# Attention kernel: who adds the causal mask to the diagonal maxima, VectorE or TensorE

## The chip, the cores and the metric

The kernel runs on one core of a Trainium2 chip. The metric is the device time of one execution in microseconds. TensorE (PE in the rows; PEld are its weight loads), VectorE (DVE), ScalarE (ACT), GpSimd (POOL) and the DMA queue of SyncE (SP) run side by side and wait for one another on semaphores.

## What is computed

One transformer layer on x of shape 4 x 2048 x 256, in float32: layer norm, causal attention with 16 heads of 16 dimensions, a residual, layer norm, a two-layer network with ternary weights and a squared ReLU, a residual. The part that matters here:

```python
qkv = x @ W_attn + b_attn
q, k, v = jnp.split(qkv, 3, axis=2)
...
scores = jnp.einsum('bhqd,bhkd->bhqk', qh, kh) * scale
causal = jnp.tril(jnp.ones((S, S), dtype=bool))
scores = jnp.where(causal, scores, -jnp.inf)
probs = jax.nn.softmax(scores, axis=-1)
out = jnp.einsum('bhqk,bhkd->bhqd', probs, vh)
```

## The kernel before

The program has four stages in a row: the preparation of the weights, the projection to q, k and v (`build_qkv`), attention (`build_attention`) and the network (`build_mlp`). Attention handles 16 units, each one batch entry and a group of `GH` = 4 heads. In a unit the queries come in `NCH` = 4 chunks of `CH` = 512.

The softmax needs the maximum of each query's row before the exponentials. So the scores are formed twice. Once they are formed with the queries across the partitions, into `ps_m`, only to find the maxima. Later they are formed with the keys across the partitions, into `ps_s`, with the negated maxima as two further rows of the product; ScalarE takes the exponential of each bank of 512 columns into the ring `probs`, and TensorE multiplies `probs` by v into `ps_acc`. A float32 product with v is two instructions, so eight weight loads stand in the trace for four heads.

The maxima are found in items, listed in `MAXES` (line 88), 68 to a unit. An item fills two banks of `ps_m`, one for each head r of a pair, at partitions 0 to 47 and 64 to 111 of the array, so that the two products run at once. There are two slots of two banks (`SLOTS`), so TensorE forms item k only after VectorE is done with item k-2 (`slot_freed`). In chunk c there are 8c full items of one piece of 512 columns, and then five items on the diagonal: two for query tile 3 (one piece of 512 columns), two for query tile 2 with tile 0 (pieces of 384 and 128), and one for query tile 1 (two pieces of 256, one for each pair of heads). Below they are called D3, D2 and D1.

`reduce_max` (line 970) is VectorE's part. A full item is one `tensor_reduce` over 1024 elements. For an item on the diagonal each piece of each head takes one custom instruction that adds `mask` and takes the maximum (line 983), followed by a read of the accumulator. Before the first of them VectorE waits on `slot_freed` for its own last item, since `sums_masked` is written again.

`order` (line 117) fixes the sequence on all engines. Between two pairs of score banks stands one item, and behind it half of the product with v for the step three earlier. So TensorE's rhythm is scores, item, values. The items run `LEAD` = 40 ahead of the scores: while the scores of a unit are formed, the items are those of its last chunk and then those of the next unit. The first 40 items of the first unit run ahead of all scores (`OPENING`); here TensorE has nothing but items to form. For the last unit no items are left after its own.

The mask is made by GpSimd in the preparation (line 244). In `build_qkv` ScalarE issues `load_ones` (line 544), four DMAs, between the copies of the first transposed chunk and the root of the second chunk's layer norm (`take_root(act, 1)`).

Of the kernel before, what the change touches and what calls it, by code (L numbers as in the profile page):

```python
# [26 lines left out]
ALU = mybir.AluOpType  # L27
# [70 lines left out]
ROWS_BEHIND = 6  # L98

# [91 lines left out]
def build_prep(nc, io, keep):  # L191

    with ExitStack() as ctx:
# [42 lines left out]
        def _(pool):  # L236
# [7 lines left out]
            pool.affine_select(out=keep["mask"][:, CH - P:], in_=keep["mask"][:, CH - P:], compare_op=ALU.is_ge, fill=NEG,  # L244
                               base=0, pattern=[[-1, P]], channel_multiplier=1).then_inc(masked, 1)

# [83 lines left out]
        def _(pe):  # L330
            pe.wait_ge(loaded, 16 * 9)
            pe.wait_ge(masked, 2)
# [168 lines left out]
class Shared:  # L501
# [3 lines left out]
    def __init__(self, nc, ctx):  # L505
# [6 lines left out]
        self.ones = t.sb("ones", [ROW, ROW])  # L512
        self.ones_set, self.fixed_in = t.sem("ones_set"), t.sem("fixed_in")
# [38 lines left out]
FIXED = 2 * MROWS  # L552
# [4 lines left out]
def build_qkv(nc, io, keep, scr, sh):  # L557

    with ExitStack() as ctx:
# [96 lines left out]
        def _(act):  # L656
            norm.take_root(act, 0)
            copy_high(act, xn_t[0], ps_t, xt_ready, xt_copied, 0)
            act.wait_ge(sh.ones_set, 1)
# [67 lines left out]
def build_attention(nc, io, keep, scr, sh):  # L727

    with ExitStack() as ctx:
# [4 lines left out]
        probs, stack_in = sh.probs, sh.stack_in  # L734

        sums_masked = t.sb("sums_masked", [P, 4, CH])
        maxes = [t.sb(f"maxes{i}", [P, 2, PAIRS, TT, NCH]) for i in range(2)]
        neg_max = [t.sb(f"neg_max{i}", [P, 2, PAIRS * TT]) for i in range(2)]
        max_parts = [t.sb(f"max_parts{i}", [P, 2, MROWS, PAIRS * TT], F32R) for i in range(2)]
        max_rows = [t.sb(f"max_rows{i}", [MROWS * GH * TT, P], F32R) for i in range(2)]  # L740
# [228 lines left out]
        def _(dve):  # L969
            def reduce_max(n, k):  # L970
# [3 lines left out]
                if pieces[0][2] < c:  # L974
                    (p, tt, i, _, _), = pieces
                    last = dve.tensor_reduce(maxes[c % 2][:, :, p, tt, i], ps_m[:, 2 * slot:2 * slot + 2], AX.X, ALU.max)  # L976
                else:

                    if NM * n + k > 0:
                        dve.wait_ge(slot_freed, NM * n + k)  # L980
                    for p, tt, i, col, width in pieces:
                        for r in range(2):
                            last = dve.tensor_tensor_reduce(sums_masked[:, 2 * pieces.index((p, tt, i, col, width)) + r, 0:width], ps_m[:, 2 * slot + r, col:col + width],  # L983
                                                            keep["mask"][:, CH - width:], 1.0, NEG, ALU.add, ALU.max,
                                                            maxes[c % 2][:, r, p, tt, i:i + 1])
# [37 lines left out]
        def _(pe):  # L1023
            def form_max(n, par, k):
# [364 lines left out]
def build_layer(nc, io):  # L1389
    with ExitStack() as ctx:  # L1390
# [11 lines left out]
            "mask": t.sb("mask", [P, CH]),  # L1402
# [41 lines left out]
```

## Time and profile before

| what | us |
|---|---|
| time, median of 3 runs | 2164.73 |
| lowest, highest | 2157.74, 2168.49 |
| the profiled execution, its own time | 2183.39 |
| its span from first to last instruction | 2181.5 |
| attention with scores, one unit of sixteen | 92.1 |

The profiled execution is 0.9% longer than the median. Durations of the rows are read against its own time. In a row of the timeline stand the start, the time to the end of the last of the merged instructions, the engine, the line, the operation, the output and inputs, partitions and elements, the count and, in brackets, how long the engine had been idle and what released it. In rows of PE and PEld the shape is partitions and rows of the product, then the elements.

### The profile page before, as it was taken

The page shows a single profiled execution, that of the slowest core. Times are in us where ns is not written, and L with a number is a line of the kernel's source. Part 1 is how long each engine was busy: PE and PEld are TensorE (multiplying, and loading weights), DVE is VectorE, ACT ScalarE, POOL GpSimd, SP SyncE. Part 2 cuts the span into 40 slices and gives each one's busy share as a digit, 9 for nine tenths or more (in the row PEclk, how much of TensorE's full clock was granted, in tenths as well). Part 3 has the DMA queues.
Part 4 walks back from the last instruction along what each step waited for, and adds up shares of the span by engine and source line. Part 5 has one row for each costly group of instructions (what it writes and reads, how often), then busy time and mean ns, then how long its engine had stood idle before and what let it go on. Part 6 is the DMA issues. An engine that isn't in the chain of part 4 may idle for free. (4 is left out here: it accounts for less than half of the span.)

```text
span 2181.5 us, 45406 instructions
## 1 busy us (share of the span) xinstructions
PE 2043.4 (94%) x17133; PEld 1099.8 (50%) x17133; DVE 1878.0 (86%) x3965; ACT 1497.3 (69%) x2800; POOL 475.9 (22%) x635
## 2 busy tenths in 40 slices
PE   3999599999999999999999999999999949999998
PEld 2877244444444344444444444444444328888887
DVE  7987889999999899999999999999999218988886
ACT  1333078888888788888888888888888725555554
POOL 0000011110111111111110111101111026776674
PEclk8999579999999999999999999999999759999999
DMA  3799121211212121121311212212120022232320
GB/s 94 281 314 321 50 50 37 73 55 54 55 37 67 48 63 49 48 63 37 78 46 51 56 37 77 53 52 56 37 73 29 12 82 81 85 102 83 88 78 30
DMA packets 162363, 168.10 MB, mean 77 GB/s; under 512 B 74064, under 2 KB 102240, under 8 KB 162144
## 3 DMA queue, kind: packets, MB, share of 16 engines
q1 hardware_dynamic: 154112, 157.72, 24.6%
q10 hardware_dynamic: 8032, 7.47, 1.2%
q8 instruction: 135, 2.21, 0.4%
q14 instruction: 84, 0.69, 0.1%
HBM read 95.77 MB, written 67.63 MB: 75 GB/s over the span
## 5 line engine op out<-in xcount | busy, mean ns | idle before, releaser
L955 ACT ACTIVATE probs<-ps_s 128x512 f32<-128x512 f32 x2176 | 1181.6, 596 | 261.1 <-PE ps_s L1067 237.3
L976 DVE TENSOR_REDUCE maxes<-ps_m 128x2 f32<-128x1024 f32 x768 | 910.6, 1218 | 71.3 <-PE ps_m L1036 65.7
L1088 PE MATMUL ps_acc<-probs,vs 128*32 128x256 f32 (+1 forms) x8696 | 709.9, 399 | 14.2 <-ACT acc_sb L933 14.2
L1067 PE MATMUL ps_s<-qs,ks 50*128 50x512 f32 (+3 forms) x2560 | 579.4, 453 | 0.4 <-ACT probs L955 0.4
L1036 PE MATMUL ps_m<-ks,qs 48*128 48x512 f32 (+3 forms) x2560 | 505.9, 401 | 36.7 <-DVE maxes L983 12.9
L983 DVE CUSTOM_DVE_ANT_0 sums_masked<-ps_m,mask 128x512 f32<-128x512 f32 (+3 forms) x1024 | 446.9, 488 | 49.9 <-PE ps_m L1036 4.6
L1067 PEld LDWEIGHTS ps_s<-qs,ks 50*128 50x128 f32 x2560 | 255.5, 187 | 420.4 <-ACT probs L955 375.1
L1088 PEld LDWEIGHTS ps_acc<-probs,vs 128*32 128x32 f32 x8696 | 174.3, 109 | 329.2 <-issue 222.9
L1036 PEld LDWEIGHTS ps_m<-ks,qs 48*128 48x128 f32 x2560 | 253.1, 191 | 156.5 <-DVE maxes L983 92.5
L893 POOL TENSOR_SCALAR_AFFINE_SELECT probs<-probs 128x512 f32<-128x512 f32 x256 | 159.3, 637 | 729.2 <-ACT probs L955 725.4
L1242 POOL TENSOR_TENSOR hid<-square,hid 128x512 fp32r<-128x512 f32 x128 | 175.9, 1383 | 105.7 <-DVE square L1253 92.8
L881 POOL CAST max_parts<-neg_max 128x16 fp32r<-128x16 f32 x64 | 12.7, 198 | 604.2 <-DVE neg_max L990 604.2
L1315 ACT ACTIVATE relu<-ps_h 128x512 f32<-128x512 f32 x128 | 76.4, 597 | 90.0 <-PE ps_h L172 81.2
L1362 PE MATMUL ps_y<-w,hid 128*128 128x256 f32 x1024 | 131.9, 284 | 6.7 <-POOL hid L1242 6.7
L1362 PEld LDWEIGHTS ps_y<-w,hid 128*128 128x128 f32 x1024 | 125.4, 188 | 11.5 <-POOL hid L1242 10.1
L1253 DVE TENSOR_TENSOR square<-relu 128x512 f32<-128x512 f32 x96 | 91.0, 954 | 30.4 <-ACT relu L1315 28.8
L170 PE MATMUL ps_h<-mxn_t,w 128*128 128x512 f32 x256 | 102.6, 401 | 1.9 <-DVE mxn_t L498 1.4
L172 PE MATMUL ps_h<-mxn_t,w 128*128 128x512 f32 x256 | 101.8, 397 | 0.0
L171 PE MATMUL ps_h<-mxn_t,w 128*128 128x512 f32 x256 | 101.6, 397 | 0.0
L983 DVE DVE_READ_ACCUMULATOR2_ANT maxes<- 128x1 f32 x1024 | 84.9, 83 | 0.0
L1320 ACT ACTIVATE hid<-relu 128x512 fp32r<-128x512 f32 x128 | 81.0, 633 | 4.1
L998 DVE RECIPROCAL recip<-sums 128x16 f32<-128x16 f32 x64 | 15.6, 244 | 64.9 <-DMA sums<-acc_sb 64.9
(126 smaller groups left out, 1624.5 us busy)
## 6 DMA issues: line engine op xcount, KB each, us to landing
qs<-q_scr SPq DMA_DIRECT2D x384, 64.0 KB, 2.7
ks<-k_scr SPq DMA_DIRECT2D x384, 64.0 KB, 2.7
q_scr<-probs SPq DMA_DIRECT2D x32, 512.0 KB, 4.5
k_scr<-probs SPq DMA_DIRECT2D x32, 512.0 KB, 5.8
o_scr<-acc_sb SPq DMA_DIRECT2D x64, 256.0 KB, 2.9
v_scr<-probs SPq DMA_DIRECT2D x16, 512.0 KB, 6.3
v_dense<-v_scr SPq DMA_DIRECT2D x16, 512.0 KB, 4.5
o_in<-o_scr SPq DMA_DIRECT2D x32, 256.0 KB
```

What stands on the lines that cost most here:

```text
L170: pe.matmul(out, sh, mh, start=start, stop=False)
L171: pe.matmul(out, sh, ml, start=False, stop=False)
L172: return pe.matmul(out, sl, mh, start=False, stop=stop)
L893: pool.affine_select(out=tile, in_=tile, compare_op=ALU.is_ge, fill=0.0, base=0, pattern=[[0, GH], [1, P]], channel_multiplier=-1).then_in ...
L955: act.activation(probs[:, s % RING, x], ps_s[:, k % BANKS], ACT.Exp).then_inc(ring_taken, 1)
L976: last = dve.tensor_reduce(maxes[c % 2][:, :, p, tt, i], ps_m[:, 2 * slot:2 * slot + 2], AX.X, ALU.max)
L983: last = dve.tensor_tensor_reduce(sums_masked[:, 2 * pieces.index((p, tt, i, col, width)) + r, 0:width], ps_m[:, 2 * slot + r, col:col + w ...
L1036: last = pe.matmul(ps_m[:, 2 * slot + r, col:col + width], qs[par][rows, c, p, tt * P:(tt + 1) * P], ks[par][rows, i, p, 0:width], start=T ...
L1067: last = pe.matmul(ps_s[:, k % BANKS, at:at + width], ks[u][rows, j // TT, p, j % TT * P:(j % TT + 1) * P], qs[u][rows, c, p, q0:q0 + widt ...
L1088: last = pe.matmul(ps_acc[h * VW:(h + 1) * VW, q0:q0 + width], vs[u][:, j, h], probs[:, s % RING, h % banks_of(s), at:at + width], start=( ...
L1242: pool.tensor_tensor(hid[:, 1, m], square[:, m], hid[:, 0, m].bitcast(F32), ALU.subtract).then_inc(low_done, 1)
L1362: last = pe.matmul(ps_y[:, i, (tt % 2) * DIM:(tt % 2 + 1) * DIM], hid[:, a, m, tt * P:(tt + 1) * P], keep["w2"][:, m], start=(m == 0 and a ...
```

## The change

A helper `vector_masks(pieces)` is true for an item whose first and last piece differ in width, which is D2 alone. For D3 and D1 TensorE now adds the mask: behind the products of a piece it issues four more, which multiply an identity by the triangular mask of 128 columns, in bfloat16, and add to the last 128 columns of the piece. Since one head owns 64 partitions of the array, the 128 partitions of identity and mask are given in two halves, and each of the two heads has its own copy. The piece's accumulation is closed by the second half. VectorE then takes D3 and D1 by one `tensor_reduce` over the same 1024 elements as a full item, for D1 with four outputs a partition. D2 stays as it was.

The two tiles are cast to bfloat16 by GpSimd in the preparation, where TensorE now waits for them, and ScalarE issues eight DMAs in `build_qkv` that spread them over `ident_half` and `mask_half`. `mask` and `sums_masked` shrink from 512 to 384 columns.

```diff
+def vector_masks(pieces):
+
+    return pieces[0][4] != pieces[-1][4]
...
+            pool.wait_ge(masked, 2)
+            pool.tensor_copy(keep["ident_h"][:], keep["ident"][:])
+            pool.tensor_copy(keep["mask_h"][:], keep["mask"][:, 2 * P:]).then_inc(masked, 1)
...
-            pe.wait_ge(masked, 2)
+            pe.wait_ge(masked, 3)
...
+            for r in range(2):
+                for half in range(2):
+                    for dst, src in ((sh.ident_half, keep["ident_h"]), (sh.mask_half, keep["mask_h"])):
+                        act.dma_start(dst[ROW * r:ROW * (r + 1), half], src[ROW * half:ROW * (half + 1), :]).then_inc(sh.fixed_in, 16)
             act.wait_ge(sh.ones_set, 1)
             load_ones(act, sh, sh.ks)
             norm.take_root(act, 1)
...
-                if pieces[0][2] < c:
-                    (p, tt, i, _, _), = pieces
-                    last = dve.tensor_reduce(maxes[c % 2][:, :, p, tt, i], ps_m[:, 2 * slot:2 * slot + 2], AX.X, ALU.max)
+                if not vector_masks(pieces):
+                    (p, tt, i, _, width) = pieces[0]
+                    pairs = slice(p, pieces[-1][0] + 1)
+                    banks = ps_m[:, 2 * slot:2 * slot + 2].rearrange("q r (p x) -> q r p x", x=width)
+                    last = dve.tensor_reduce(maxes[c % 2][:, :, pairs, tt, i], banks, AX.X, ALU.max)
...
-                                         ks[par][rows, i, p, 0:width], start=True, stop=True, skip_group_check=True)
+                                         ks[par][rows, i, p, 0:width], start=True, stop=(i < c or vector_masks(pieces)), skip_group_check=True)
+                    if i == c and not vector_masks(pieces):
+                        for half in range(2):
+                            for r in range(2):
+                                rows = slice(ROW * r, ROW * (r + 1))
+                                last = pe.matmul(ps_m[:, 2 * slot + r, col + width - P:col + width], ident_half[rows, half],
+                                                 mask_half[rows, half], start=False, stop=(half == 1), skip_group_check=True)
```

On TensorE, in the scores of a unit's chunk 2, the items D1 of its last chunk and the first D3 of the next unit stood like this before (`ps_s` are scores, `ps_m` the item, `ps_acc` the values):

```order
L1067 MATMUL ps_s<-qs,ks 128x512 x2
L1036 MATMUL ps_m<-ks,qs 128x256 x4
L1088 MATMUL ps_acc<-probs,vs 32x256 x4
L1067 MATMUL ps_s<-qs,ks 128x512 x2
L1036 MATMUL ps_m<-ks,qs 128x512 x2
L1088 MATMUL ps_acc<-probs,vs 32x256 x4
```

The same two items now:

```order
L1090 MATMUL ps_s<-qs,ks 128x512 x2
L1053 MATMUL ps_m<-ks,qs 128x256 x2
L1059 MATMUL ps_m<-mask_half,ident_half 128x128 x4
L1053 MATMUL ps_m<-ks,qs 128x256 x2
L1059 MATMUL ps_m<-mask_half,ident_half 128x128 x4
L1111 MATMUL ps_acc<-probs,vs 32x256 x4
L1090 MATMUL ps_s<-qs,ks 128x512 x2
L1053 MATMUL ps_m<-ks,qs 128x512 x2
L1059 MATMUL ps_m<-mask_half,ident_half 128x128 x4
L1111 MATMUL ps_acc<-probs,vs 32x256 x4
```

D1 has eight further products and D3 four, and all of them stand between the scores and the values.

On VectorE, item D1 with the full item and the chunk's last step behind it, before (an ISA row is a custom instruction or a read of its accumulator):

```order
L983 ISA sums_masked,maxes<-ps_m,mask 128x256
L983 ISA maxes 128x1
L983 ISA sums_masked,maxes<-ps_m,mask 128x256
L983 ISA maxes 128x1
L983 ISA sums_masked,maxes<-ps_m,mask 128x256
L983 ISA maxes 128x1
L983 ISA sums_masked,maxes<-ps_m,mask 128x256
L983 ISA maxes 128x1
L976 TENSOR_REDUCE maxes<-ps_m 128x2
L990 TENSOR_REDUCE neg_max<-maxes 128x16
```

And now:

```order
L993 TENSOR_REDUCE maxes<-ps_m 128x4
L993 TENSOR_REDUCE maxes<-ps_m 128x2
L1007 TENSOR_REDUCE neg_max<-maxes 128x16
```

Eight instructions became one with four outputs a partition.

On ScalarE's queue, between the first transposed chunk and the second chunk's root in `build_qkv`, before:

```order
L491 CAST xn_t<-ps_t 128x512 x2
L549 DMA ks<-ones 1x64x64 x4
L428 ACTIVATE root_attn<-var_attn 128x4
L583 DMA x<-in_L_attn_x 128x4x256
L491 CAST xn_t<-ps_t 128x512 x2
```

And now, with the eight transfers of identity and mask ahead of those of the ones:

```order
L499 CAST xn_t<-ps_t 128x512 x2
L673 DMA ident_half<-ident_h 64x128
L673 DMA mask_half<-mask_h 64x128
...
L559 DMA ks<-ones 1x64x64 x4
L436 ACTIVATE root_attn<-var_attn 128x4
```

The root, and the load of the third chunk of x behind it, come after twelve issues instead of four.

## Rows read from the trace of the kernel before

**Rows 1.** The page: busy time of each engine, share of the span, instructions.
```profile
PE 2043.4 (94%) x17133; PEld 1099.8 (50%) x17133; DVE 1878.0 (86%) x3965; ACT 1497.3 (69%) x2800; POOL 475.9 (22%) x635
```

**Rows 2.** Windows, one unit and the opening: PE, PEld, DVE, ACT, POOL, clock, DMA, GB/s.
```profile
925.00:1017.10 92.10, 90.43 (x873) 37.93 (x871) 85.31 (x185) 76.12 (x145) 12.58 (x25) 1.00 0.21 54
...
222.00:272.00 50.00, 31.45 (x100) 13.46 (x102) 47.27 (x115) 0.51 (x2) 2.34 (x5) 0.50 0.07 25
```

**Rows 3.** Waits in the same unit, 925 to 1017: total, times, longest.
```profile
PEld ps_m L1036 <- DVE maxes L983: 4.9, 12, 0.8
...
PEld ps_m L1036 <- DVE maxes L976: 2.3, 4, 0.8
```

**Rows 4.** Timeline of the weight loads, a stretch in which TensorE doesn't wait for VectorE.
```profile
1013.78 0.19 PEld L1067 LDWEIGHTS ps_s<-qs,ks 50*128 50x128 f32 x2 [0.41 <-ACT probs L955]
1013.89 0.43 PEld L1036 LDWEIGHTS ps_m<-ks,qs 48*128 48x128 f32 x4
1014.46 0.16 PEld L1088 LDWEIGHTS ps_acc<-probs,vs 128*32 128x32 f32 x8
1015.03 0.30 PEld L1067 LDWEIGHTS ps_s<-qs,ks 50*128 50x128 f32 x4 [0.41 <-ACT probs L955]
```

**Rows 5.** Timeline of the weight loads, around the diagonals of chunks 3 and 0.
```profile
963.08 0.20 PEld L1067 LDWEIGHTS ps_s<-qs,ks 50*128 50x128 f32 x2 [0.41 <-ACT probs L955]
...
971.16 0.30 PEld L1036 LDWEIGHTS ps_m<-ks,qs 48*128 48x128 f32 x4 [0.43 <-DVE maxes L983]
...
972.16 0.18 PEld L1067 LDWEIGHTS ps_s<-qs,ks 50*128 50x128 f32 x2 [0.41 <-ACT probs L955]
...
972.76 0.19 PEld L1036 LDWEIGHTS ps_m<-ks,qs 48*128 48x128 f32 x2 [0.42 <-DVE maxes L983]
...
973.98 0.18 PEld L1067 LDWEIGHTS ps_s<-qs,ks 50*128 50x128 f32 x2 [0.41 <-ACT max_rows L925]
...
975.38 0.19 PEld L1067 LDWEIGHTS ps_s<-qs,ks 50*128 50x128 f32 x2 [0.41 <-ACT probs L955]
```

**Rows 6.** The same, around the diagonal of chunk 1.
```profile
988.48 0.29 PEld L1067 LDWEIGHTS ps_s<-qs,ks 50*128 50x128 f32 x2 [0.20 <-issue]
...
993.43 0.19 PEld L1067 LDWEIGHTS ps_s<-qs,ks 50*128 50x128 f32 x2 [0.41 <-ACT probs L955]
```

**Rows 7.** The same, behind the diagonal of chunk 2.
```profile
1019.19 0.38 PEld L1067 LDWEIGHTS ps_s<-qs,ks 50*128 50x128 f32 x2
1019.87 0.19 PEld L1036 LDWEIGHTS ps_m<-ks,qs 48*128 48x128 f32 x2 [0.30 <-DVE maxes L983]
```

**Rows 8.** Timeline of VectorE: full items, then the diagonal of chunk 3.
```profile
928.88 4.69 DVE L976 TENSOR_REDUCE maxes<-ps_m 128x2 f32<-128x1024 f32 x4
...
958.99 0.69 DVE L983 CUSTOM_DVE_ANT_0 sums_masked<-ps_m,mask 128x512 f32<-128x512 f32 x1
...
961.89 0.56 DVE L983 CUSTOM_DVE_ANT_0 sums_masked<-ps_m,mask 128x384 f32<-128x384 f32 x1
...
965.12 0.42 DVE L983 CUSTOM_DVE_ANT_0 sums_masked<-ps_m,mask 128x256 f32<-128x256 f32 x1
...
966.73 0.69 DVE L983 CUSTOM_DVE_ANT_0 sums_masked<-ps_m,mask 128x512 f32<-128x512 f32 x1
```

**Rows 9.** Timeline of TensorE in the projection: products of 256 columns.
```profile
206.15 0.28 PE L170 MATMUL ps_v<-w_qkv,xn_t 128*128 128x256 f32 x1
...
206.97 0.28 PE L171 MATMUL ps_v<-w_qkv,xn_t 128*128 128x256 f32 x1
```

**Rows 10.** Timeline of the start: GpSimd's mask, TensorE's first product, ScalarE's queue.
```profile
1.95 0.29 POOL L244 TENSOR_SCALAR_AFFINE_SELECT mask<-mask 128x128 f32<-128x128 f32 x1
...
13.67 1.88 PE L334 MATMUL ps_prep<-ident,u_in 128*16 128x128 f32 x8 [13.67 <-DMA b_qk<-in_L_attn_b_attn]
...
47.40 2.47 ACTq L549 DMA_DIRECT2D ks<-ones  x4
...
50.78 0.20 ACT L428 ACTIVATE root_attn<-var_attn 128x4 f32<-128x4 f32 x1 [2.80 <-DVE var_attn L408]
```

More of the change, by code:

```diff
@@ L242, in _ @@
                                base=0, pattern=[[-1, P]], channel_multiplier=1)
-            pool.affine_select(out=keep["mask"][:, CH - P:], in_=keep["mask"][:, CH - P:], compare_op=ALU.is_ge, fill=NEG,
+            pool.affine_select(out=keep["mask"][:, 2 * P:], in_=keep["mask"][:, 2 * P:], compare_op=ALU.is_ge, fill=NEG,
                                base=0, pattern=[[-1, P]], channel_multiplier=1).then_inc(masked, 1)
+            pool.wait_ge(masked, 2)
+            pool.tensor_copy(keep["ident_h"][:], keep["ident"][:])
+            pool.tensor_copy(keep["mask_h"][:], keep["mask"][:, 2 * P:]).then_inc(masked, 1)
         @block.vector
@@ L512, in __init__ @@
         self.ones = t.sb("ones", [ROW, ROW])
+        self.ident_half = t.sb("ident_half", [P, 2, P], BF16)
+        self.mask_half = t.sb("mask_half", [P, 2, P], BF16)
         self.ones_set, self.fixed_in = t.sem("ones_set"), t.sem("fixed_in")
@@ L549, in load_ones @@
             act.dma_start(ks[row:row + 1].bitcast(F32).rearrange("o c p (x e) -> o (c p x) e", e=ROW), sh.ones[:]).then_inc(sh.fixed_in, 16)
-FIXED = 2 * MROWS
+FIXED = 2 * MROWS + 2 * 2 * 2
 PRELOAD, PRELOADED = 8, 4
@@ L733, in build_attention @@
         vs = [sh.vs, t.sb("vs1", [P, KT, GH, VW])]
-        probs, stack_in = sh.probs, sh.stack_in
-        sums_masked = t.sb("sums_masked", [P, 4, CH])
+        probs, ident_half, mask_half, stack_in = sh.probs, sh.ident_half, sh.mask_half, sh.stack_in
         maxes = [t.sb(f"maxes{i}", [P, 2, PAIRS, TT, NCH]) for i in range(2)]
@@ L739, in build_attention @@
         max_parts = [t.sb(f"max_parts{i}", [P, 2, MROWS, PAIRS * TT], F32R) for i in range(2)]
+        sums_masked = t.sb("sums_masked", [P, 4, 3 * P])
         max_rows = [t.sb(f"max_rows{i}", [MROWS * GH * TT, P], F32R) for i in range(2)]
@@ L980, in reduce_max @@
                         dve.wait_ge(slot_freed, NM * n + k)
-                    for p, tt, i, col, width in pieces:
+                    for x, (p, tt, i, col, width) in enumerate(pieces):
                         for r in range(2):
-                            last = dve.tensor_tensor_reduce(sums_masked[:, 2 * pieces.index((p, tt, i, col, width)) + r, 0:width], ps_m[:, 2 * slot + r, col:col + width],
-                                                            keep["mask"][:, CH - width:], 1.0, NEG, ALU.add, ALU.max,
+                            last = dve.tensor_tensor_reduce(sums_masked[:, 2 * x + r, 0:width], ps_m[:, 2 * slot + r, col:col + width],
+                                                            keep["mask"][:, 3 * P - width:], 1.0, NEG, ALU.add, ALU.max,
                                                             maxes[c % 2][:, r, p, tt, i:i + 1])
@@ L1401, in build_layer @@
             "ident": t.sb("ident", [P, P]),
-            "mask": t.sb("mask", [P, CH]),
+            "ident_h": t.sb("ident_h", [P, P], BF16),
+            "mask_h": t.sb("mask_h", [P, P], BF16),
+            "mask": t.sb("mask", [P, 3 * P]),
         }
```

## The prediction

> **What bounds the kernel now.** I read the page first, for the busy engines. TensorE shows 94% and VectorE 86% [rows 1], so a step that takes work from one and gives it to the other can go either way, and the share of the span doesn't tell which. Next I read one unit of attention by windows. Sixteen of them make up most of the time. In the 92.1 us of a unit TensorE is busy for 90.43, VectorE for 85.31 and ScalarE for 76.12, at a granted clock of 1.00, which is the level of 2.4 GHz [rows 2]. The busy time of matmuls is modelled over waits, so I went on to the waits: the weight loads of items wait for VectorE 16 times in that unit, 4.9 + 2.3 = 7.2 us together [rows 3]. That is the ceiling of what a faster VectorE can give back; most of it stands behind the custom instructions of the diagonal.
>
> Then the timeline, for TensorE's own rhythm. Where nothing holds it, scores, item and values follow at 0.11, 0.57 and 0.57 us, hence 1.24 us (1.25 by the rounded row) from one load of scores to the next [rows 4]. Where an item waits for VectorE, the next loads come 1.00 us behind the item's instead of 1.14 [rows 4, 5]. So a wait costs nothing until the item's load is 0.11 + 0.14 = 0.25 us behind the scores', and everything beyond.
>
> On VectorE four full items take 4.69 us, less the tail of about 0.08 that overlaps the next, hence 1.15 each. D3 takes (961.89 - 958.99) / 2 = 1.45, D2 (965.12 - 961.89) / 2 = 1.61 and D1 966.73 - 965.12 = 1.61 [rows 8]. A full item is shorter than TensorE's 1.24; every item of the diagonal is longer. Chunks 3 and 0 follow each other, ten such items in a row, and TensorE has only two slots. This is what the stall looks like: between 963.08 and 975.38 there are eight intervals of scores, 12.30 us in all [rows 5]. Eight at 1.24 are 9.92, and the transposition of the row maxima in one of them is 0.22 (973.98 - 972.76 = 1.22 instead of 1.00) [rows 5]. So 2.16 us are lost there. Around the diagonal of chunk 1 three intervals take 993.43 - 988.48 = 4.95 instead of 3.72, so 1.23 are lost [rows 6]. Behind the diagonal of chunk 2 an item's load is 0.68 behind the scores', so 0.43 are lost [rows 7]. Together 3.82 us a unit, of a ceiling of 7.2; the rest are waits inside the free 0.25, and waits after bursts of items at the short steps, which stay.
>
> **The change part by part.**
>
> VectorE. D3 and D1 become one reduction of 1024 elements. The trace has no reduction with four outputs, but the same count from the same banks, so I take 1.15. A chunk's diagonal gets shorter by 2 x (1.45 - 1.15) + (1.61 - 1.15) = 1.06 us. The ten items of chunks 3 and 0 then need 4 x 1.61 + 6 x 1.15 = 13.3 us where TensorE alone needs 12.4. With TensorE's new work added (below, 13.5 to 13.9) VectorE is no longer the later one. So all of the 3.82 us goes, and what is late next is TensorE itself.
>
> TensorE. Each piece gets two pairs of products of 128 columns, and the two heads of a pair run at once. Products of 256 columns follow each other at (206.97 - 206.15) / 7 = 0.117 us [rows 9], so a pair of 128 columns streams in 0.06. A second pair of weight loads lies 0.30 - 0.19 = 0.11 us behind the first [rows 5]; it hides behind 256 or more columns, as an item of two pieces costs no more than one of 512 (0.57 again) [rows 4]. It doesn't hide behind 128 columns. The trace has no load of bfloat16 weights, so I bound it: from above by this 0.11, from below by the stream of 0.06, at which it is hidden. At 0.11, D3 costs 0.11 + 0.06 = 0.17: the first mask pair has to stand until the second's weights are in. D1 costs 0.11 + 0.11 + 0.11 + 0.06 = 0.39, the second 0.11 being the wait for the weights of the second piece. A chunk costs 2 x 0.17 + 0.39 = 0.73. At 0.06 the same steps give 0.12 for D3 and 0.06 + 0.11 + 0.06 + 0.06 = 0.29 for D1, and 0.53 for a chunk. I take the middle, since bfloat16 weights are half the bytes but no row shows that this shortens the load.
>
> Where VectorE sets the end of a stretch now, this work lies beside it; once VectorE is faster, it lies on the path, so I charge all of it. By stage of a unit, with loads at 0.11 and at 0.06: chunks 3 and 0 gain 2.16 - 1.46 = 0.70 or 2.16 - 1.06 = 1.10; chunk 1 gains 1.23 - 0.73 = 0.50 or 0.70; chunk 2, whose items stand in a stretch where TensorE never waits [rows 4], loses 0.43 - 0.73 = -0.30 or -0.10. That is 0.90 or 1.70 a unit and, for the 15 units that have a successor, 13.5 or 25.5 us. The last unit has only its chunk 3 diagonal left and loses 0.7 or 0.5.
>
> The opening. In its 50 us VectorE is busy for 47.27 [rows 2], so here the whole of its saving counts. Three diagonals lie in the first 40 items: 3 x 1.06 = 3.2 us. The clock is granted at 0.50 there (1.2 GHz), so a mask pair streams in twice 0.06, but TensorE is idle for over a third of it.
>
> The start. The two casts on GpSimd come 2.2 us into the program, and TensorE's first product waits for a DMA until 13.67 [rows 10]: that wait hides them. Without it they would cost two instructions of some 0.3 us. The eight DMAs aren't hidden so well. Four issues take 2.47 us on ScalarE's queue, so eight take 4.9. Behind them wait the root of the second chunk, for which VectorE holds up the normalisation and TensorE its transposes and the first chunk's products, and the load of the third chunk of x. The queue was free at 49.87 and the root ran at 50.78, so 0.9 is slack and 4.0 us are lost [rows 10]. The projection is busy throughout afterwards, so I see nothing that gives it back; the bounds are 0 and 5.
>
> Sum: 13.5 - 0.7 + 3.2 - 4.0 = 12.0 us gained with loads at 0.11, and 25.5 - 0.5 + 3.2 - 4.0 = 24.2 with loads at 0.06. The middle is 18 us, 0.83% of the profiled execution's 2183.39. Off the median of 2164.73 that gives 2147.
>
> **The rivals.**
>
> *Fast loads.* If a bfloat16 load is never longer than its 0.06 of stream, the gain is 24 us and the time 2141. For it: half the bytes. Against it: the float32r loads of the same 128 columns show 0.11 whatever the number of rows.
> By the Trainium skill's page "TensorE: Matmul & The Clock Gate", under "Weight-path perf modes", weights that are 128 wide and not FP32 load by a fast path, about twice as fast as measured there. By that rule this rival is the one to come true. Its section "LDWEIGHTS (loading the stationary operand)" gives columns / 1.2, an estimate of 107 ns, and the trace's 0.11 agrees with that for float32r.
>
> *The array has to empty between the two kinds of product.* From an item to the values the array changes from two products side by side to one over all 128 partitions. In a stalled item 0.43 us lie between the two loads, of which 0.11 is the item's load and 0.23 its 512 columns, so 0.09 is spent on the change, and the next load can't be hidden [rows 4, 5, 9]. If a change between float32r and bfloat16 costs the same, each is 0.09 + 0.11 = 0.20. D3 then costs 0.20 + 0.11 + 0.06 = 0.37, D1 0.37 + 0.20 + 0.37 = 0.94 and a chunk 1.68. The gain turns into 15 x (3.82 - 6.72) - 1.7 + 3.2 - 4.0 = -46 us, so 2210. It decides from 0.93 us a chunk, or 0.12 a pair: 15 x (3.82 - 4 x 0.93) - 0.93 + 3.2 - 4.0 is about nothing. Against it: the mask products keep the 64-partition halves of the items, and from scores (50 rows) to an item (48 rows) nothing is lost.
> The page "TensorEngine Tiling (Array Packing)" of the Trainium skill says under "Key Properties" that a change of tiling mode drains the array, not a change of tile; it says nothing of formats. The trace agrees on the mode.
>
> *ScalarE takes the room.* Scores also wait for their banks, which ScalarE frees. It is busy 76.12 of 92.1 us [rows 2]. If it takes back 0.5 us at chunk 1 and 0.5 at chunks 3 and 0, 15 of the 18 us are lost and the time is 2162. For it: the scores' loads carry ScalarE as their releaser throughout [rows 4 to 6]. Against it: that wait of 0.41 is there in the undisturbed rhythm too and costs nothing, and two exponentials fit into 1.24.
>
> **How the numbers follow.** The forecast, a gain of 12 to 24, has a chance of 0.55; fast loads, or a little better, 0.15; ScalarE 0.17; the emptied array 0.13. A measurement of this kernel can tell about 0.5%, here 11 us. Faster by more than that: most of the forecast's 0.55, whose lower end lies at that bound, and nearly all of the fast loads, 0.60 together. Within it: the rest of the forecast and most of ScalarE's case, 0.25. Slower: the emptied array, and a small share of ScalarE's case with a dear load, 0.15. The range goes from 2132, the fast loads with the start hidden and 5 us for the median's own spread, to 2170, ScalarE's case with the loads at their upper price. It leaves out the emptied array.
>
> **What would show it.** VectorE's reductions with four outputs at 1.15 us, and no wait of an item's load on VectorE of 0.4 in the ten items of chunks 3 and 0. Scores' loads there 1.24 us apart at full items, about 1.38 at D3 and 1.58 at D1. A unit of about 90.8 us instead of 92.1. The opening shorter by 3 us. The second root of the start at about 54.8 instead of 50.78, and the end of the projection later by 4. I am wrong if the mask pairs lie 0.12 us or more apart on average, if the reduction with four outputs is longer than 1.24, or if the scores' intervals don't shrink although VectorE is ahead.

## The result, and the profile after

| | before | after |
|---|---|---|
| median of 10 runs, us | 2165.55 | 2147.28 |
| lowest, highest | 2157.74, 2176.32 | 2143.43, 2168.99 |
| profiled execution, its own time | 2183.39 | 2144.52 |
| its span | 2181.5 | 2142.8 |
| mean granted clock of TensorE over that span | 0.958 | 0.970 |
| one unit of attention, median of 14 | 92.11 | 90.89 |

The ratio is 0.9911, with a 95% interval from 0.9883 to 0.994: the changed kernel is 0.9% faster, within a us of the forecast. The two profiled executions lie 39 us apart, twice as far as the medians, and the row of the clock goes with that (the last section sets the time against the clock), so I compare units and not those two times.

The page of the kernel after, busy time of each engine, answers to [rows 1]. VectorE has 29 us less work and TensorE 1024 products more:

```profile
PE 2021.7 (94%) x18157; PEld 1121.5 (52%) x18157; DVE 1849.4 (86%) x3133; ACT 1494.7 (70%) x2800; POOL 474.8 (22%) x637
```

Windows of the kernel after, one unit and the opening, as in [rows 2] (PE, PEld, DVE, ACT, POOL, clock, DMA, GB/s):

```profile
1095.83:1186.71 90.88, 90.14 (x936) 39.43 (x934) 83.45 (x132) 76.04 (x144) 12.56 (x25) 1.00 0.21 55
222.00:272.00 50.00, 33.97 (x148) 15.37 (x146) 46.09 (x83) 0.51 (x2) 2.65 (x5) 0.55 0.14 50
```

The waits of the same unit answer to [rows 3]. Item loads wait for VectorE for 3.1 + 0.2 = 3.3 us instead of 7.2, and nearly nothing is left behind the custom instructions (L1000, once L983):

```profile
PEld ps_m L1053 <- DVE maxes L993: 3.1, 5, 0.8
...
PEld ps_m L1053 <- DVE maxes L1000: 0.2, 1, 0.2
```

The groups of instructions by shape (busy us, mean ns | idle before). A reduction with four outputs takes 1221 ns, one with two 1220, and the next instruction starts 1.14 us behind either (medians of those that follow without a pause):

```profile
L993 DVE TENSOR_REDUCE maxes<-ps_m 128x2 f32<-128x1024 f32 x896 | 1067.6, 1220 | 102.3 <-PE ps_m L1053 80.3 <-PE ps_m L1059 8.5
...
L993 DVE TENSOR_REDUCE maxes<-ps_m 128x4 f32<-128x1024 f32 x64 | 78.1, 1221 | 0.0
...
L1059 PEld LDWEIGHTS ps_m<-mask_half,ident_half 64*128 64x128 bf16 x1024 | 32.3, 98 | 42.4 <-issue 37.6
```

The timeline of the weight loads in the stretch of chunk 2's diagonal, a plain item and the first D3, then the D1, as in [rows 4] (L1090 is the scores, L1053 the item, L1059 the mask, L1111 the values):

```profile
1176.92 0.19 PEld L1053 LDWEIGHTS ps_m<-ks,qs 48*128 48x128 f32 x2
1177.48 0.16 PEld L1111 LDWEIGHTS ps_acc<-probs,vs 128*32 128x32 f32 x8 [0.37 <-ACT probs L970]
1178.05 0.19 PEld L1090 LDWEIGHTS ps_s<-qs,ks 50*128 50x128 f32 x2 [0.41 <-ACT probs L970]
1178.16 0.20 PEld L1053 LDWEIGHTS ps_m<-ks,qs 48*128 48x128 f32 x2
1178.63 0.12 PEld L1059 LDWEIGHTS ps_m<-mask_half,ident_half 64*128 64x128 bf16 x4 [0.28 <-issue]
1178.86 0.16 PEld L1111 LDWEIGHTS ps_acc<-probs,vs 128*32 128x32 f32 x8
...
1182.32 0.30 PEld L1053 LDWEIGHTS ps_m<-ks,qs 48*128 48x128 f32 x4
1182.76 0.16 PEld L1111 LDWEIGHTS ps_acc<-probs,vs 128*32 128x32 f32 x8
1183.32 0.30 PEld L1090 LDWEIGHTS ps_s<-qs,ks 50*128 50x128 f32 x4 [0.41 <-ACT probs L970]
1183.61 0.19 PEld L1053 LDWEIGHTS ps_m<-ks,qs 48*128 48x128 f32 x2
...
1184.36 0.16 PEld L1111 LDWEIGHTS ps_acc<-probs,vs 128*32 128x32 f32 x8
```

From the item's load to the values' it was 1177.48 - 1176.92 = 0.56. With D3's mask it is 1178.86 - 1178.16 = 0.70. At this D1 the item's loads come later behind the scores' (0.29 instead of 0.11), and the D2 just ahead, which has no mask product, takes 1182.76 - 1182.32 = 0.44; D1 takes 1184.36 - 1183.61 = 0.75, which is 0.31 more. Over all items behind the opening the medians are 0.56 for full items, 0.69 for D3 and 0.87 for D1 (0.88 in chunks 3 and 0, 0.75 in 1 and 2): the mask costs 0.13 at D3 and 0.31 at D1, 2 x 0.13 + 0.31 = 0.57 a chunk and 2.28 a unit.

Around the diagonals of chunks 3 and 0, the timeline that answers to [rows 5]:

```profile
1131.37 0.19 PEld L1090 LDWEIGHTS ps_s<-qs,ks 50*128 50x128 f32 x2 [0.41 <-ACT probs L970]
...
1132.93 0.19 PEld L1090 LDWEIGHTS ps_s<-qs,ks 50*128 50x128 f32 x2 [0.41 <-ACT probs L970]
...
1134.29 0.19 PEld L1090 LDWEIGHTS ps_s<-qs,ks 50*128 50x128 f32 x2 [0.41 <-ACT probs L970]
...
1135.66 0.19 PEld L1090 LDWEIGHTS ps_s<-qs,ks 50*128 50x128 f32 x2 [0.41 <-ACT probs L970]
...
1136.90 0.19 PEld L1090 LDWEIGHTS ps_s<-qs,ks 50*128 50x128 f32 x2 [0.41 <-ACT probs L970]
...
1142.59 0.18 PEld L1090 LDWEIGHTS ps_s<-qs,ks 50*128 50x128 f32 x2 [0.41 <-ACT probs L970]
```

The intervals are 1.56 at D1, 1.36 and 1.37 at D3, then 1.24 at D2. Eight of them, one with the transposition, take 1142.59 - 1131.37 = 11.22 where they took 12.30. No item load there waits for VectorE any more.

Where the time went, by the load times of the items in the two profiled executions. In both, item 40, where the first unit's scores begin, stands at 273.32 us: the start is 3.25 longer (first item 225.10, before 221.85) and the opening 3.25 shorter (48.22 instead of 51.47). The 15 unit periods behind it are 24.0 shorter, of which 15 x 1.22 = 18.3 is the unit itself and the rest is in two units that ran longer before at a lower clock (98.01 against 94.10, 95.16 against 90.85). The last unit's items take the same in both (35.64 and 35.63 from its item 40 to its last). From the last item to the last product with v, before needs 14.7 more (64.04 against 49.34). Windows over that stretch, first two of before, then one of after, show the same engines with the clock at 0.57 and 0.52, near the level of 1.2 GHz, against 1.00:

```profile
1720.00:1740.00 20.00, 19.43 (x125) 6.09 (x128) 0.25 (x1) 13.35 (x27) 0.00 (x0) 0.57 0.05 15
1740.00:1765.00 25.00, 25.00 (x162) 7.66 (x158) 0.00 (x0) 14.04 (x26) 2.50 (x4) 0.52 0.00 1
```

```profile
1700.00:1727.00 27.00, 26.70 (x258) 10.76 (x256) 0.25 (x1) 23.20 (x45) 2.50 (x4) 1.00 0.04 12
```

What follows the last product with v takes 416.5 us in both.

### The profile page after: what moved, and what is told of

Read it like the earlier page. It is cut to its first block and busy times, and to the rows that moved or that the text cites. A ratio compares the mean times of both kernels' runs of the same rounds, so it can differ in the third digit from the quotient of the medians.

```text
span 2142.8 us, 46441 instructions
## 1 busy us (share of the span) xinstructions
PE 2021.7 (94%) x18157; PEld 1121.5 (52%) x18157; DVE 1849.4 (86%) x3133; ACT 1494.7 (70%) x2800; POOL 474.8 (22%) x637
## 5 line engine op out<-in xcount | busy, mean ns | idle before, releaser
L993 DVE TENSOR_REDUCE maxes<-ps_m 128x2 f32<-128x1024 f32 (+1 forms) x960 | 1142.1, 1220 | 102.3 <-PE ps_m L1053 80.3
L1111 PE MATMUL ps_acc<-probs,vs 128*32 128x256 f32 (+1 forms) x8696 | 695.8, 392 | 12.1 <-ACT acc_sb L948 12.1
L1090 PE MATMUL ps_s<-qs,ks 50*128 50x512 f32 (+3 forms) x2560 | 573.4, 446 | 0.9 <-ACT probs L970 0.9
L1053 PE MATMUL ps_m<-ks,qs 48*128 48x512 f32 (+3 forms) x2560 | 503.6, 392 | 16.7 <-DVE maxes L993 9.9
L1090 PEld LDWEIGHTS ps_s<-qs,ks 50*128 50x128 f32 x2560 | 254.0, 184 | 410.5 <-ACT probs L970 374.3
L1111 PEld LDWEIGHTS ps_acc<-probs,vs 128*32 128x32 f32 x8696 | 172.9, 108 | 294.3 <-issue 188.9
L1053 PEld LDWEIGHTS ps_m<-ks,qs 48*128 48x128 f32 x2560 | 262.9, 191 | 91.9 <-DVE maxes L993 71.9
L1000 DVE CUSTOM_DVE_ANT_0 sums_masked<-ps_m,mask 128x384 f32<-128x384 f32 (+1 forms) x512 | 186.6, 421 | 20.1 <-PE ps_m L1053 4.0
L1059 PE MATMUL ps_m<-mask_half,ident_half 64*128 64x128 bf16 x1024 | 77.4, 226 | 0.0
L499 ACT CAST mxn_t<-mps_t 128x512 fp32r<-128x512 f32 x32 | 17.3, 590 | 70.7 <-PE mps_t L1375 70.7
```

The source lines that it names most:

```text
L993: last = dve.tensor_reduce(maxes[c % 2][:, :, pairs, tt, i], banks, AX.X, ALU.max)
L1000: last = dve.tensor_tensor_reduce(sums_masked[:, 2 * x + r, 0:width], ps_m[:, 2 * slot + r, col:col + width], keep["mask"][:, 3 * P - widt ...
L1090: last = pe.matmul(ps_s[:, k % BANKS, at:at + width], ks[u][rows, j // TT, p, j % TT * P:(j % TT + 1) * P], qs[u][rows, c, p, q0:q0 + widt ...
L1111: last = pe.matmul(ps_acc[h * VW:(h + 1) * VW, q0:q0 + width], vs[u][:, j, h], probs[:, s % RING, h % banks_of(s), at:at + width], start=( ...
```

## The experiments

Every time has the clock's spread in it, so each kernel is judged by its unit first, the period from item 40 of a unit to item 40 of the next. A is the stretch of thirteen items around the diagonals of chunks 3 and 0, B the ten around chunk 1's, C the nine around chunk 2's; the rest of a unit is 47.2 us in all twelve kernels. A, B and C are medians of 13 units, the unit of 14, in us; the first item is that of the one profiled execution. Ratios are against the kernel before, timed beside each, since its median moved from 2165.55 to 2179.57 between the sets of runs. For e6 and e7, whose profiled executions had a low mean clock (0.956 and 0.957), the three stretches and the rest add up to 91.36 and 90.99, 0.16 and 0.14 less than the median unit; for the others the sum meets the unit within 0.07.

| kernel | unit | A | B | C | first item | median time | ratio, interval |
|---|---|---|---|---|---|---|---|
| before | 92.11 | 19.01 | 13.43 | 12.48 | 221.85 | 2165.55 | |
| after | 90.89 | 17.91 | 12.95 | 12.81 | 225.10 | 2147.28 | 0.991, 0.988 to 0.994 |
| e1, no mask products | 89.48 | 17.34 | 12.68 | 12.24 | 227.24 | 2145.35 | 0.982, 0.974 to 0.990 |
| e2, they alone | 92.46 | 19.00 | 13.41 | 12.80 | 226.01 | 2180.52 | 1.001, 0.998 to 1.005 |
| e3, mask in float32r | 91.42 | 18.18 | 13.07 | 12.97 | 229.34 | 2170.18 | 0.998, 0.993 to 1.002 |
| e4, other queue | 90.94 | 17.91 | 12.95 | 12.81 | 219.68 | 2142.96 | 0.985, 0.979 to 0.990 |
| e5, e4 and chunk 2 by VectorE | 90.57 | 17.93 | 12.95 | 12.48 | 222.05 | 2149.23 | 0.988, 0.983 to 0.993 |
| e6, D1 alone | 91.52 | 18.53 | 13.04 | 12.59 | 224.51 | 2166.08 | 0.998, 0.994 to 1.002 |
| e7, D3 alone | 91.13 | 17.98 | 13.32 | 12.49 | 226.36 | 2156.90 | 0.995, 0.991 to 0.999 |
| e8, D2 too | 93.02 | 19.18 | 13.17 | 13.45 | 224.03 | 2185.11 | 1.007, 1.002 to 1.011 |
| e9, e5 with less mask | 90.20 | 17.63 | 12.89 | 12.48 | 219.98 | 2134.17 | 0.981, 0.977 to 0.986 |
| e10, mask twice | 92.34 | 18.58 | 13.33 | 13.24 | 227.87 | 2192.43, one run | |

**e1_no_mask_products: what VectorE's part alone is worth.**

```diff
-                    if i == c and not vector_masks(pieces):
+                    if False:
                         for half in range(2):
```

The maxima are then taken over unmasked scores, so they are upper bounds; a common shift leaves a softmax the same, but nothing here measures a row whose masked scores lie far above its others.

> Leaves out the mask products on TensorE for D3 and D1, so their maxima are taken over unmasked scores; VectorE's part is that of the changed kernel. It measures the price of the mask products where they stand. My account (stalls on VectorE gone, then TensorE pays 0.13 for D3 and 0.31 for D1 on its own path, 2.28 us a unit): a unit falls from 90.9 to between 88.6 and 89.1 us, the time to between 2112 and 2119. Rival, ScalarE takes the room: a unit stays at 90 or more and the time above 2134.

The unit is 89.48, above my account's 88.6 to 89.1 and below the rival's 90. The median time of 2145.35 is far above the 2112 to 2119 that I expected, with clocks of 0.952 to 0.969; the one run at 0.969 took 2124.52, where the seven of the kernel before at 0.969 took 2161.60 to 2166.41, about 40 us or 15 x 2.63. So the faster VectorE brings 92.11 - 89.48 = 2.63 and not 3.82, and putting the mask products in costs 90.89 - 89.48 = 1.41 of the 2.28 that they take. My account had the net gain about right and each of its two parts too large. The timeline of its weight loads shows what is left. First the second D3 of chunk 3, then D1 of chunk 0 and the full item behind it:

```profile
1120.90 0.29 PEld L1053 LDWEIGHTS ps_m<-ks,qs 48*128 48x128 f32 x2
1121.92 0.19 PEld L1111 LDWEIGHTS ps_acc<-probs,vs 128*32 128x32 f32 x8 [0.73 <-ACT probs L970]
...
1131.20 0.19 PEld L1090 LDWEIGHTS ps_s<-qs,ks 50*128 50x128 f32 x2 [0.41 <-ACT probs L970]
1131.57 0.30 PEld L1053 LDWEIGHTS ps_m<-ks,qs 48*128 48x128 f32 x4 [0.19 <-DVE maxes L1000]
...
1132.57 0.19 PEld L1090 LDWEIGHTS ps_s<-qs,ks 50*128 50x128 f32 x2 [0.41 <-ACT probs L970]
1133.18 0.19 PEld L1053 LDWEIGHTS ps_m<-ks,qs 48*128 48x128 f32 x2 [0.42 <-DVE maxes L1000]
```

Behind the two D2, still 1.61 each on VectorE, the loads of the next two items are 0.37 and 0.61 behind the scores': VectorE is the later one again. And where TensorE comes out of a run of short steps, the values' load is 1.02 behind the item's instead of 0.56. The load's row names an exponential as what released it. The rows of ScalarE and of the products show what came last: ScalarE's copy of the accumulator `ps_acc`, which follows a row of exponentials without a pause. The same happens at the D1 of chunk 1, here with the scores' loads ahead and behind:

```profile
1118.54 2.79 ACT L970 ACTIVATE probs<-ps_s 128x512 f32<-128x512 f32 x5
1121.22 0.59 ACT L948 COPY acc_sb<-ps_acc 128x512 f32<-128x512 f32 x1
1121.95 0.64 PE L1111 MATMUL ps_acc<-probs,vs 128*32 128x256 f32 x8 [0.32 <-ACT acc_sb L948]
...
1148.76 0.27 PEld L1090 LDWEIGHTS ps_s<-qs,ks 50*128 50x128 f32 x2 [0.20 <-issue]
...
1149.17 0.59 ACT L948 COPY acc_sb<-ps_acc 128x512 f32<-128x512 f32 x1
1149.91 0.64 PE L1111 MATMUL ps_acc<-probs,vs 128*32 128x256 f32 x8 [0.26 <-ACT acc_sb L948]
1150.48 0.18 PEld L1090 LDWEIGHTS ps_s<-qs,ks 50*128 50x128 f32 x2 [0.41 <-ACT probs L970]
```

Mask products that stand in such a place take the place of a wait. The items' load times (medians of 13 units) say which do. The two D3 of chunk 3 take 2.81 us together in e1, in the kernel after and in the kernel before: their 0.26 lie under the first copy. D1 of chunk 1 takes 1.61 in e1 and in the kernel after: its 0.31 lie under the second, so B pays 0.27 of 0.57. Another 0.31 of A lie where e1 waits for VectorE's D2. C pays its 0.57 in full (12.24 to 12.81). Together some 0.87 us a unit aren't paid.

**e2_mask_products_alone: TensorE's part alone, VectorE as before.** The mask is added twice, which changes no maximum.

```diff
-                if not vector_masks(pieces):
+                if pieces[0][2] < c:
...
-                                                            keep["mask"][:, 3 * P - width:], 1.0, NEG, ALU.add, ALU.max,
+                                                            keep["mask"][:, CH - width:], 1.0, NEG, ALU.add, ALU.max,
```

> TensorE adds the mask for D3 and D1 as in the changed kernel, but VectorE still takes all items of the diagonal by its custom instructions as before and adds the mask once more. It does one half of the change alone. My account (the price is hidden while VectorE is late, and paid in full only in the stretch of chunk 2's diagonal): a unit of 92.7 to 93.3 us against 92.1 before, the time 12 to 21 us above before with the 3.3 us of the start. Rival, the price is paid everywhere: a unit of 94.4 and 37 us above before.

The unit grows by 0.35 only, less than the 0.6 to 1.2 that I expected, and the median time is 5 us above before's and not 12 to 21. A and B don't change (19.00 and 13.41): where VectorE sets the pace, 1.7 us of TensorE's new work lie beside its waits. C pays 0.32 of 0.57, where I had expected it in full. With the later start this is 15 x 0.35 + 4 = 9 us, or 0.4%, inside the interval that was measured.

**e3_mask_in_float32r: does the weight load set the price?** The same products with four-byte operands.

```diff
-        self.ident_half = t.sb("ident_half", [P, 2, P], BF16)
-        self.mask_half = t.sb("mask_half", [P, 2, P], BF16)
+        self.ident_half = t.sb("ident_half", [P, 2, P], F32R)
+        self.mask_half = t.sb("mask_half", [P, 2, P], F32R)
```

> Identity and mask as float32r instead of bfloat16, nothing else. Tells whether the load of the weights sets the price of a pair. My account (a float32r load is 0.11 us, a bfloat16 one is hidden under the 0.06 of stream): D3 costs 0.17 or more and D1 0.39, a unit of 91.5 us against 90.9, the time 8 to 12 us above the changed kernel, near 2157. Rival, the stream and a change of format set the price: float32r saves the change of format, a unit of 90.9 or less and the time 2147 or less.

As expected, 91.42. (The median time of 2170.18 is 23 above that of the kernel after, but with clocks down to 0.955; its two runs at 0.970 took 2154.08 and 2154.33, some 10 above the kernel after at 0.970 or 0.971, where 8 to 12 were expected.) Item to values is 0.73 at D3 and 0.96 at D1, so the mask costs 0.17 and 0.40, which are the prediction's sums with loads of 0.11. Its groups by shape and its timeline:

```profile
L1059 PEld LDWEIGHTS ps_m<-mask_half,ident_half 64*128 64x128 f32 x1024 | 94.4, 194 | 10.8
```

```profile
1198.73 0.19 PEld L1053 LDWEIGHTS ps_m<-ks,qs 48*128 48x128 f32 x2
1198.97 0.42 PEld L1059 LDWEIGHTS ps_m<-mask_half,ident_half 64*128 64x128 f32 x4
1199.47 0.16 PEld L1111 LDWEIGHTS ps_acc<-probs,vs 128*32 128x32 f32 x8
```

A load has a mean of 194 ns here and 98 in bfloat16. It also starts earlier, 0.24 us behind the item's load and under its stream, where the bfloat16 load starts 0.47 behind it (0.23 and 0.47 are the medians of 122 D3). As I read it, that head start is why so large a difference in the load makes only 0.04 us at D3; no run separates the two.

**e4_spread_from_sync_queue: the eight DMAs on the other queue.** The same loop, moved from ScalarE to SyncE.

```diff
             load(sp, 1, 1)
+            for r in range(2):
+                for half in range(2):
+                    for dst, src in ((sh.ident_half, keep["ident_h"]), (sh.mask_half, keep["mask_h"])):
+                        sp.dma_start(dst[ROW * r:ROW * (r + 1), half], src[ROW * half:ROW * (half + 1), :]).then_inc(sh.fixed_in, 16)
```

> The eight DMAs of identity and mask are issued from SyncE's queue behind the first two loads of x, not from ScalarE's. My account (the issues delay the second root, and nothing gives that back): the first item at 221.9 us instead of 225.1 and the time 3.3 us lower, near 2144. Rival, the projection's end is set by its transfers: the first item stays at 225 and the time at 2147.

ScalarE's timeline at the start, of the kernel after and then of e4:

```profile
48.16 0.53 ACTq L673 DMA_DIRECT2D ident_half<-ident_h  x1
...
52.59 0.62 ACTq L673 DMA_DIRECT2D mask_half<-mask_h  x1
53.25 2.55 ACTq L559 DMA_DIRECT2D ks<-ones  x4
55.85 0.20 ACT L436 ACTIVATE root_attn<-var_attn 128x4 f32<-128x4 f32 x1 [7.11 <-issue]
```

```profile
48.02 2.46 ACTq L559 DMA_DIRECT2D ks<-ones  x4
51.40 0.20 ACT L436 ACTIVATE root_attn<-var_attn 128x4 f32<-128x4 f32 x1 [2.80 <-DVE var_attn L416]
```

Eight issues took 5.1 us and the root came 4.5 later than without them. At the first item the difference is 5.4. In time it is less: of runs at a granted clock of 0.970 or 0.971, e4's three have the median 2142.25 and after's six 2144.6, hence 2.4 us, less than the 3.3 expected. Among all kernels with the issues on ScalarE the first item lies between 224.0 and 229.3, in those without between 219.7 and 222.1, with medians about 5 apart. So the start costs some 2 to 5 us, and one execution doesn't settle it.

**e5_chunk_2_by_vector: e4, and chunk 2's diagonal back on VectorE behind the first unit.**

```diff
-def vector_masks(pieces):
+def vector_masks(pieces, n=0):
-    return pieces[0][4] != pieces[-1][4]
+    return pieces[0][4] != pieces[-1][4] or (n > 0 and pieces[0][2] == 2)
```

> From the second unit on, D3 and D1 of chunk 2 go back to VectorE's custom instructions; the other chunks keep the mask on TensorE; the eight DMAs stay on SyncE's queue. My account (in chunk 2's stretch TensorE is the later engine, so the mask products only cost there, 0.33 us): a unit of 90.5 to 90.6 us against 90.9, the time 5 us below that of the DMAs on SyncE's queue alone, near 2138. Rival: VectorE's backlog from chunk 2 is paid again in the next chunk 3 items, and a unit stays at 90.9 or more.

C is 12.48 again, A stays at 17.93, and the unit is 90.57, as expected: VectorE's backlog isn't paid again in the next stretch. The median time isn't the expected 2138 but 2149.23, at clocks of 0.958 to 0.973. Chunk 2 is the one place where the change loses.

**e6_d1_alone and e7_d3_alone: one of the two items each.** The other stays with VectorE, and as in e5 `mask` is 512 columns wide again and full items keep their reduction.

```diff
-    return pieces[0][4] != pieces[-1][4]
+    return pieces[0][4] != pieces[-1][4] or len(pieces) == 1
```

> Only D1 gets its mask from TensorE, D3 is done as before. My account, item by item with VectorE's 1.45 and TensorE's 0.31: chunks 3 and 0 gain 0.6, chunk 1 gains 0.4, chunk 2 loses up to 0.1, a unit of 91.1 to 91.2 us. If the gains of D1 and D3 simply added up, D1 with the larger saving (0.46 of 1.06 a chunk, at 0.31 of 0.57) would bring less than half of the 1.22, a unit above 91.5.

```diff
-    return pieces[0][4] != pieces[-1][4]
+    return len(pieces) > 1
```

> Only D3 gets its mask from TensorE, D1 is done as before. My account, item by item with TensorE's 0.13 for D3: chunks 3 and 0 gain 0.9, chunk 1 gains 0.2, chunk 2 loses 0.1 to 0.2, a unit of 91.1 to 91.3 us. If the gains added up, D3 would bring 1.22 less what D1 alone brings, so at my value for D1 only 0.3, a unit of 91.8.

D1 alone gains 0.59 by the unit (0.76 by the stretches), less than the 0.9 to 1.0 expected, and D3 alone 0.98 (1.13 by the stretches), as expected. Together they gain 1.22 and not 1.57 or more. The stretches show why. In A, D3 alone brings 1.03 of the 1.10 and D1 0.48: the same wait is removed by either. In B it is D1 that counts, 0.39 of 0.48. In C they cost 0.11 and 0.01 alone and 0.33 together.

**e8_all_by_tensor: D2 too, with one reduction for each of its pieces.**

```diff
-    return pieces[0][4] != pieces[-1][4]
+    return False
...
+                    if width != pieces[-1][4]:
+                        for p, tt, i, col, width in pieces:
+                            last = dve.tensor_reduce(maxes[c % 2][:, :, p, tt, i], ps_m[:, 2 * slot:2 * slot + 2, col:col + width], AX.X, ALU.max)
```

> D2 gets its mask from TensorE too, and VectorE takes it by two reductions of 768 and 256 elements, about 1.2 us instead of 1.61. My account: VectorE has no stall left to remove except 0.1 or 0.2 a unit, and TensorE pays 0.31 for each of eight D2 items, so a unit of 92.8 to 93.4 us, the time above before's. Rival, VectorE's speed still counts in the diagonals: a unit of 90.9 or less.

93.02, as expected, and 0.7% slower than before. At D2 item to values is 0.88, so its mask costs 0.32 and a chunk 0.57 + 0.64 = 1.21. Here the mask's price exceeds the stall: 1.21 is above the 0.93 a chunk at which the prediction said that the exchange turns, and the change with its 0.57 is below.

**e9_half_wide_mask: e5, with fewer columns and the mask products at the end of an item.** The second half of the triangle has nothing in its first 64 columns, so half the products shrink to 64. D1's mask products come behind both pieces.

```diff
-                    if i == c and not vector_masks(pieces, n):
-                        for half in range(2):
+                if pieces[0][2] == c and not vector_masks(pieces, n):
+                    for half in range(2):
+                        for p, tt, i, col, width in pieces:
...
-                                last = pe.matmul(ps_m[:, 2 * slot + r, col + width - P:col + width], ident_half[rows, half],
-                                                 mask_half[rows, half], start=False, stop=(half == 1), skip_group_check=True)
+                                first = ROW * half
+                                last = pe.matmul(ps_m[:, 2 * slot + r, col + width - P + first:col + width], ident_half[rows, half],
+                                                 mask_half[rows, half, first:], start=False, stop=(half == 1), skip_group_check=True)
```

> On top of e5: the second half of the mask is zero in its first 64 columns, so its products take only the last 64; and D1 forms both pieces before any mask product. My account (TensorE's price falls from 0.13 to about 0.10 for D3 and from 0.31 to about 0.20 for D1, and most of it counts): a unit of 90.2 to 90.4 us against 90.57, the time at equal clock 3 to 5 us below e5. Rival, the bfloat16 load sets the price and narrower products bring nothing: a unit of 90.5 or more.

90.20, as expected, and the lowest median time of all, 2134.17, 1.9% below the kernel before. (e1, with the lower unit, was timed at lower clocks.) Its weight loads at a D1 and a D3:

```profile
1128.74 0.43 PEld L1053 LDWEIGHTS ps_m<-ks,qs 48*128 48x128 f32 x4
1129.20 0.24 PEld L1061 LDWEIGHTS ps_m<-mask_half,ident_half 64*128 64x128 bf16 x8
1129.50 0.16 PEld L1113 LDWEIGHTS ps_acc<-probs,vs 128*32 128x32 f32 x8
...
1130.17 0.19 PEld L1053 LDWEIGHTS ps_m<-ks,qs 48*128 48x128 f32 x2
...
1130.84 0.16 PEld L1113 LDWEIGHTS ps_acc<-probs,vs 128*32 128x32 f32 x8
```

D1 takes 0.76 and D3 0.67 from item to values, by the medians 0.19 and 0.10 for the mask instead of 0.31 and 0.13. The order and the columns change together here, and no run separates them. D3, whose order is the same, saves 0.03 by one narrowed pair; by that, D1's two narrowed pairs are about 0.06 of its 0.12 and the order is the rest (an estimate).

**e10_mask_twice: every mask product issued twice.** What is added to the masked places is doubled, which leaves every maximum as it is.

```diff
-                        for half in range(2):
+                        for half in (0, 0, 1, 1):
```

> The changed kernel with every mask product issued twice. It tells how much of TensorE's price lies on the path. My account (the first 0.57 a chunk used up the room that VectorE's remaining lateness left, what is added counts in full, 0.12 for D3 and 0.24 for D1): a unit of 92.6 to 93.0 us against 90.9. Rival, a fixed share of about 0.6 counts whatever is added: a unit of 92.0.

The unit is 92.34, between the two theories. Item to values at a D3:

```profile
1205.40 0.19 PEld L1053 LDWEIGHTS ps_m<-ks,qs 48*128 48x128 f32 x2
1205.86 0.23 PEld L1059 LDWEIGHTS ps_m<-mask_half,ident_half 64*128 64x128 bf16 x8 [0.27 <-issue]
1206.19 0.16 PEld L1111 LDWEIGHTS ps_acc<-probs,vs 128*32 128x32 f32 x8
```

0.79, by the medians 0.80 and 1.10 at D1, which is 0.11 and 0.23 more than in the kernel after: 0.055 for each further pair, the 0.06 that 128 columns stream. That makes 1.8 us a unit, of which 1.45 or 80% show. Of e3's extra 0.17 x 4 = 0.68 it is 0.53 or 78%. So the first 2.28 us of mask work are paid to 62%, and what comes on top to 80%: most of the waits that hide it are used up. By stretch, A pays 0.67 of 0.90, B 0.38 of 0.45 and C 0.43 of 0.45. What A doesn't pay is at the two D3 of chunk 3, which still take 2.81 us together: the wait for the copy of the accumulator covers these 0.23 too.

## Why the prediction held, point by point

- **VectorE's reduction.** Right. Four outputs cost what two cost (1221 and 1220 ns), and 1.14 us from start to start where 1.15 was said. In the opening, where VectorE has the whole say, the 3.2 us came out as 3.25 (51.47 to 48.22; e2, with VectorE as before, has 51.7; D1 alone has 49.9 and D3 alone 49.7, where 3 x 0.46 and 3 x 0.60 less are due).
- **The price of a mask pair.** Right in its bounds, 0.53 to 0.73 a chunk, and it is 0.57, close to the lower end. The middle that I took was 0.06 too high. The rival of fast loads had the price right: a load of bfloat16 weights hides under 0.06 us of stream, since each further pair costs 0.055 (e10). It missed the time of 2141 by the stall, next point. The Trainium skill's page "TensorE: Matmul & The Clock Gate", under "Weight-path perf modes", gives 128-wide weights that are not FP32 a load about twice as fast; the trace agrees, 98 ns against e3's 194 for float32r, which it doesn't name.
- **"So all of the 3.82 us goes."** This step failed. The faster VectorE is worth 2.63 by e1. I held every interval over 1.24 us for a wait on VectorE that would vanish. In A e1 gains 1.67 of 2.16; the rest is VectorE's lateness at D2, which the mask products of the real change then fill (12.30 to 11.22 is what the sum with 0.06 gives). In B e1 gains 0.75 of 1.23. The 0.48 left are one interval of scores, 1150.48 - 1148.76 = 1.72 instead of 1.24, and there the values wait for ScalarE's copy of the accumulator. It lies behind a run of short steps, and the two exponentials of a step take 2 x 0.596 = 1.19 us on ScalarE, so steps of 1.09 can't go on: that wait was due anyway. In C e1 gains 0.24 of 0.43.
- **"I charge all of it."** This failed too, the other way: 1.41 of 2.28 are on the path. By stretch, forecast with loads at 0.11 and 0.06, then measured: A 0.70 or 1.10, and 1.10; B 0.50 or 0.70, and 0.48; C -0.30 or -0.10, and -0.33. The unit was to gain 0.90 to 1.70 and gained 1.22. That the middle of 1.30 is so near is luck: 1.19 too much of stall (3.82 - 2.63) stands against 1.11 too much of price, since 2.52 was charged, four chunks at 0.63, and 1.41 was paid.
- **The start.** The issues cost what was said (5.1 us for eight, 4.9 expected; root at 55.85, 54.8 expected). The 4.0 at the first item came out as 3.25 in this pair of executions, and as 2 to 5 over all.
- **The sum.** 15 x 1.22 + 3.25 - 3.25 is 18.3. The last unit was to lose 0.5 to 0.7; up to its last item it loses nothing, and the mask of that item, D1, can cost at most 0.31 behind it. The medians say 18.3 and the forecast was 18.
- **The rival of the emptied array** is refuted by the trace: it needed 0.37 at D3 and 0.94 at D1 and the trace shows 0.13 and 0.31. Going between float32r and bfloat16 within the same halves of the array costs nothing that the rows show.
- **The rival of ScalarE** isn't what happened, since its unit would have been 91.8. Its mechanism is there on a small scale, by the copy of the accumulator and not by the banks of scores. At the D3 of chunk 3 the wait (1.02 - 0.56 = 0.46 us) is in the kernel before too. At the D1 of chunk 1 ScalarE does take room that VectorE gives up, the 0.48 above. Both help the change on the other side: they are the waits under which mask products lie.

What stays open: what the 0.19 us are that e1 leaves in C. There the item's load is 0.23 behind the scores', inside the free 0.25. And no run took ScalarE's copies away, so that they are the wait in B is read from the trace and not tested.

## What to carry to other kernels

Work that is moved from one engine to another has two prices, and each has to be read where it lands: what the relieved engine gives back is less than the sum of its waits as soon as a third engine is close behind, and what the other engine takes is less than its instructions' time as long as it still waits there. Ask it stretch by stretch, and give the work back where a stretch only pays (chunk 2 here). And where small products with weights of their own are added to a group, try the cheaper weight format (0.57 against 0.74 us a chunk here), and then both fewer columns and a place together at the group's end (0.39 a chunk in e9, by the two at once).

## What the runs showed of the hardware

- The time of one and the same kernel follows the mean granted clock of TensorE. The 63 executions of the kernel before that were timed beside the experiments lie between 2158.14 and 2190.48 us. At 0.955 stand 2187.68 and 2188.79, at 0.971 five from 2159.15 to 2163.59 and at 0.972 2158.14: about 1.8 us for each 0.001. At one value of the clock up to 8 us are left over (2182.61 to 2190.48 at 0.957). In the profiled execution the drops sit in the opening (0.50 in [rows 2]), in the first unit (0.88 over its 98 us), shortly in the fifth (0.96) and behind the last item (0.52 and 0.57). Why they come at one place in one execution and not in the next stays open. So a difference of half a per cent between two kernels is shown by the unit period, or by runs at the same clock, sooner than by medians.
- Weight loads of 128 columns: in bfloat16 98 ns each by the profile, and 0.055 us for each further pair of products (e10); in float32r 194 ns (e3), and 0.11 from one pair of loads to the next [rows 5]. Behind the load of an item of 512 columns in float32r the first bfloat16 load starts 0.47 us later, the first float32r load 0.24 us.
- Gains don't add: 0.59 for D1 and 0.98 for D3 made 1.22.
- The releaser that a row of a weight load names isn't always the one that came last: the load at 1121.92 names an exponential, the products behind it the copy of the accumulator.
